# Edge loop of a graph-attention kernel: VectorE adds the gathered rows to the second pair of scores in five of seven steps, and GpSimd's gathers wait for their ring slot alone

## What is computed

```python
src, dst = (edge_index[0], edge_index[1])
x_l = (x @ W_l.T + b_l).reshape(n, HEADS, DIMS)
x_r = (x @ W_r.T + b_r).reshape(n, HEADS, DIMS)
...
e_feat = (e_attr @ W_e.T).reshape(-1, HEADS, DIMS)
s = x_l[src] + x_r[dst] + e_feat
s = jax.nn.leaky_relu(s, NEG_SLOPE)
alpha = jnp.einsum('ehc,hc->eh', s, att)
amax = jax.ops.segment_max(alpha, dst, num_segments=n)
ex = jnp.exp(alpha - amax[dst])
denom = jax.ops.segment_sum(ex, dst, num_segments=n)
alpha = ex / (denom[dst] + 1e-16)
out = jax.ops.segment_sum(alpha[..., None] * x_l[src], dst, num_segments=n)
```

## Time and profile before

| what | value |
|---|---|
| median of 3 launches | 3488.56 us (3485.78 to 3489.42) |
| the profiled execution's own time | 3486.59 us |
| its span, first to last instruction | 3484.9 us |
| scores of the edge loop (L1311), first to last start | 148.5 to 1379.1 us |
| PE busy, share of the span | 3136.0 us, 90% |
| DVE | 1877.1 us, 54% |
| ACT | 1357.1 us, 39% |
| POOL | 1244.5 us, 36% |
| L1311 matmuls, 1680 records | 522.2 us |
| L1312 matmuls, 960 + 720 records | 293.0 + 220.8 us |
| L1294 gathers, 480 + 360 | 461.4 + 345.2 us |

### The profile page before, as it was taken

One profiled execution on the slowest core, in us unless ns is written; L12 is line 12 of the kernel. 1 busy time (PEld: TensorE's weight loads), 2 busy tenths in 40 slices (PEclk: granted clock), 3 DMA queues, 4 the chain that ended last, 5 costly groups with the idle time before them and its releaser, 6 DMA issues. The chain is left out here.

```text
span 3484.9 us, 52064 instructions
## 1 busy us (share of the span) xinstructions
PE 3136.0 (90%) x14323; PEld 2542.8 (73%) x14324; DVE 1877.1 (54%) x3779; ACT 1357.1 (39%) x4647; POOL 1244.5 (36%) x1197
## 2 busy tenths in 40 slices
PE   2799999999999999557998899889989986999988
PEld 1577777777777777346777677767767775888877
DVE  5577877777777877865436343643454340111002
ACT  0047767767777766431223122222312211222232
POOL 2276666666666664113103010300020016000016
PEclk9899999999999999678999999999989978999999
DMA  5576776677676676251101011000000043333333
GB/s 135 155 190 167 168 167 167 164 165 166 166 166 164 166 167 131 78 183 30 30 14 34 23 34 36 8 1 14 27 37 1 1 128 104 113 123 123 115 113 107
DMA packets 301651, 355.64 MB, mean 102 GB/s; under 512 B 164806, under 2 KB 223771, under 8 KB 297545
## 3 DMA queue, kind: packets, MB, share of 16 engines
q0 software_dynamic: 67472, 178.15, 20.1%
q1 hardware_dynamic: 233510, 173.64, 18.8%
q10 hardware_dynamic: 560, 2.35, 0.2%
HBM read 298.03 MB, written 54.91 MB: 101 GB/s over the span
## 5 line engine op out<-in xcount | busy, mean ns | idle before, releaser
L1311 PE MATMUL a_pS<-g_xr,a_lt 128*128 x1680 | 522.2, 393 | 28.0 <-DMA XS<-xl_d,a_ix 22.9
L1294 POOL DMA_INDIRECT a_g<-xl_d,a_ix x480 | 461.4, 961 | 222.4 <-PE a_pS L1312 135.0
L1405 ACT ACTIVATE b_m<-a_g,c_pcx 128x64 f32<-128x64 f32 x1856 | 454.6, 333 | 0.0
L1319 PE MATMUL b_pM<-b_m,b_oh 128*112 128x281 f32 x1680 | 445.3, 404 | 5.3 <-DVE g_acc L1447 3.5
L1440 DVE SCALAR_TENSOR_TENSOR a_r<-a_pS,g_attx 128x528 f32<-128x528 f32 x420 | 296.6, 706 | 243.8 <-PE a_pS L1312 234.8
L1294 POOL DMA_INDIRECT XS<-xl_d,a_ix x360 | 345.2, 959 | 135.3 <-issue 91.5
L113 POOL TENSOR_TENSOR m_rstd<-m_ve,m_mhalf 125x5 f32<-125x5 f32 x45 | 53.1, 1180 | 928.4 <-DVE m_ve L103 919.9
L1311 PEld LDWEIGHTS a_pS<-g_xr,a_lt 128*128 128x128 f32 x1680 | 310.0, 191 | 90.2 <-issue 33.3
L1319 PEld LDWEIGHTS b_pM<-b_m,b_oh 128*112 128x112 f32 x1680 | 292.1, 177 | 102.1 <-issue 11.4
L421 PE MATMUL m_pH<-m_h,m_w 128*128 128x312 f32 (+1 forms) x1280 | 341.9, 428 | 7.7 <-DVE m_h L566 7.7
L1405 ACT ACTIVATE b_m<-XS,c_pcx 128x64 f32<-128x64 f32 x1424 | 348.5, 333 | 0.0
(11 more groups left out here) (371 smaller groups left out, 4410.0 us busy)
## 6 DMA issues: line engine op xcount, KB each, us to landing
a_db<-dl_d SPq DMA_DIRECT2D x212, 224.0 KB
f_w<-in_ffn_W1p SPq DMA_DIRECT2D x32, 1024.0 KB
m_w<-in_mix_W SPq DMA_DIRECT2D x8, 1024.0 KB
f_w<-in_ffn_W2p SPq DMA_DIRECT2D x8, 1024.0 KB
a_g<-xl_d,a_ix POOLq DMA_INDIRECT x480, 5.7
xg_d<-m_zero POOLq DMA_DIRECT2D x1, 7168.0 KB, 30.5
a_lt<-eat_d SPq DMA_DIRECT2D x214, 32.0 KB, 4.1
eat_d<-a_stage SPq DMA_DIRECT2D x15, 448.0 KB
```

The source lines that it names most:

```text
L1294: p.indirect_dma_start(out=gathered(t)[:, j, :], out_offset=None, in_=xl_d, in_offset=bass.IndirectOffsetOnAxis(ap=IX[:, t // BSTEPS, n:n ...
L1311: pe.matmul(o, lt[:, j, :], XRW[:, bass.ds(ws[h], 1), :].rearrange("p a d -> p (a d)"), start=True, stop=False)
L1319: ins = pe.matmul(pM[0:WN, h, 0:MW], OH[:, b, j, :], M[:, b, j, :], start=(j == 2 * h), stop=(j == 2 * h + 1))
L1405: ins = a.activation(m[:, j, part], gathered(ts)[:, j, part], ACT.Copy, scale=of[:, first + j, h, 0:1])
```

## The change

In the steps with tau 2 to 6, `scores(1)` leaves out the identity matmuls of items 2 and 3. VectorE then reads the PSUM pair, adds the gathered rows and writes `R` (`lift`), and later gates `R` in place (`lifted_gate`). The semaphore that lets TensorE write the pair again is given by `lift` (renamed `a_read1`). The two waits of the gathers for scores are gone, with `AHEAD`. The chain at tau 0 and 1, `scores(0)` and `sums` stay.

```diff
-AHEAD = 3
+LIFTED = (2, 3, 4, 5, 6)
...
                         for j in range(IG):
                             n = IG * (t % BSTEPS) + j
-                            if j % 2 == 0:
-                                wait(p, f"a_scored{j // 2}", base, t + 1 - AHEAD)
-                                p.sem_inc(s["a_seen"], 1)
                             p.indirect_dma_start(out=gathered(t)[:, j, :], out_offset=None, in_=xl_d,
...
                         def scores(h, ws):
-                            wait(pe, f"a_gated{h}", base, t)
+                            lifted = h == 1 and t % BSTEPS in LIFTED
+                            wait(pe, f"a_read{h}", base, t)
                             for j in (2 * h, 2 * h + 1):
                                 o = pS[0:TE, j, 0:GD]
-                                pe.matmul(o, lt[:, j, :], XRW[:, bass.ds(ws[h], 1), :].rearrange("p a d -> p (a d)"), start=True, stop=False)
-                                ins = pe.matmul(o, ident[:, :], gathered(t)[:, j, :], start=False, stop=True)
+                                ins = pe.matmul(o, lt[:, j, :], XRW[:, bass.ds(ws[h], 1), :].rearrange("p a d -> p (a d)"), start=True, stop=lifted)
+                                if not lifted:
+                                    ins = pe.matmul(o, ident[:, :], gathered(t)[:, j, :], start=False, stop=True)
...
+                        def lift():
+                            v.wait_ge(s[f"a_g{t}"], 64 * i + 64)
+                            wait(v, "a_scored1", base, t + 1)
+                            v.tensor_tensor(R[:, 2:4, :], pS[0:TE, 2:4, 0:GD], gathered(t)[:, 2:4, :], ALU.add).then_inc(s["a_read1"], 1)
...
+                        def lifted_gate():
+                            wait(v, "a_read1", base, t + 1)
+                            v.scalar_tensor_tensor(out=R[:, 2:4, :], in0=R[:, 2:4, :], scalar=0.0,
+                                                   in1=attx[:, :].unsqueeze(1).broadcast_to([TE, 2, GD]), op0=ALU.max, op1=ALU.mult).then_inc(s["a_gated"], 1)
...
-                        if scoring:
+                        if scoring and lifted:
+                            lift()
+                        elif scoring:
                             gate(1)
...
+                        if scoring and lifted:
+                            lifted_gate()
...
                         if scoring:
-                            wait(v, "a_gated1", base, t + 1)
+                            wait(v, "a_read1", base, t + 1)
+                            if lifted:
+                                v.wait_ge(s["a_gated"], 2 * len(LIFTED) * i + len([k for k in range(t + 1) if k % BSTEPS in LIFTED]))
```

More of the change, by code:

```diff
@@ L1436, in slot @@
                         scores = pA[0:CP, 0:TE]
+                        lifted = t % BSTEPS in LIFTED
+                        def lift():
+                            v.wait_ge(s[f"a_g{t}"], 64 * i + 64)
+                            wait(v, "a_scored1", base, t + 1)
+                            v.tensor_tensor(R[:, 2:4, :], pS[0:TE, 2:4, 0:GD], gathered(t)[:, 2:4, :], ALU.add).then_inc(s["a_read1"], 1)
                         def gate(h):
@@ L1440, in gate @@
                             v.scalar_tensor_tensor(out=R[:, 2 * h:2 * h + 2, :], in0=pS[0:TE, 2 * h:2 * h + 2, 0:GD], scalar=0.0,
-                                                   in1=attx[:, :].unsqueeze(1).broadcast_to([TE, 2, GD]), op0=ALU.max, op1=ALU.mult).then_inc(s[f"a_gated{h}"], 1)
+                                                   in1=attx[:, :].unsqueeze(1).broadcast_to([TE, 2, GD]), op0=ALU.max, op1=ALU.mult).then_inc(s[f"a_read{h}"], 1)
+                        def lifted_gate():
+                            wait(v, "a_read1", base, t + 1)
+                            v.scalar_tensor_tensor(out=R[:, 2:4, :], in0=R[:, 2:4, :], scalar=0.0,
+                                                   in1=attx[:, :].unsqueeze(1).broadcast_to([TE, 2, GD]), op0=ALU.max, op1=ALU.mult).then_inc(s["a_gated"], 1)
                         def add(h, at):
```

## The result

The changed kernel takes 3448.18 us (median of 4, 3447.56 to 3455.33) against 3487.59 for the kernel before (median of 4): the ratio is 0.9892, with a 95% interval of 0.9875 to 0.9909. So it is faster, by 39 us where 85 were forecast. The profiled execution took 3455.33 us, the longest of the four, with a span of 3453.6; that of before was 3486.59, with a span of 3484.9. The gain between the two profiled spans is 31.3 us, less than the 39 of the medians, and all of it lies in the edge loop: the last scores start at 1346.5 us instead of 1379.1.

A forecast was written before the change was run, and what follows sets the result against it. TensorE bounds the kernel; a batch falls from 41.54 to 38.35 us, 28 × 3.19 = 89 us, less 4 for late gathers: 3486.59 less 85 is 3401.6, plus 2 for the median, 3403 us; range 3369 to 3456.

The forecast's parts named there:

- TensorE bound before; ten matmuls a batch, 4.45 us: Edge loop: TensorE sets the pace; ten matmuls at 0.445 us leave each batch, 41.54 to 37.09 us.
- `lift` for the gate, and the lifted gate: VectorE, lifted steps: the lift replaces a gate at 692 ns, adding nothing; the new gate takes 698 ns, adding 3.1 us a batch.
- The half-rate rival: The new gate's two fp32 SBUF inputs stream at half rate, 2.75 us more a batch; 3474 us, chance 0.02.
- VectorE's five steps, 26.1 us: Tau 2 to 6: VectorE needs 25.3 to 26.9 us, middle 26.1, more than TensorE's 24.15.
- The term for the dependence: The reduce must see the finished gate: 0.34 us at tau 4, 5 and 6, 0.7 to 1.2 us a batch.
- The wait at the transpose: Tau 0: TensorE waits for VectorE's reduce before transposing the batch's scores, 1.26 us once a batch.
- The removed waits for scores cost nothing: GpSimd's gathers: their 125.7 us of waits for scores only show GpSimd being ahead, a lead TensorE can't use.
- The gathers: GpSimd supply: 1.26 us a gather, 5.04 a step, 73.1 us a round, against 76.7 forecast for two batches.
- late landings: Gathered rows that arrive late for TensorE: 0.15 us a batch, 4 us in all.
- The place: The narrowest place for gather supply is behind the attribute gathers, at step 2, with 2.1 us to spare.
- The one for supply or clock: Late gathers or a lower TensorE clock after waits take back gain: about 3426 to 3452 us, chance 0.26 together.
- The one of contention between VectorE and GpSimd: SBUF contention lengthens the new gates; at 2.0 us each, 92 us more, 3581 us; chance 0.05.

The follow-up runs named there:

- e5: The changed kernel without the gather of item 3 from the second round on, so three gathers a step; 3387.73 us, ratio 0.9707.
- e1: The kernel before with the gathers' waits for scores taken out and no lift; 3491.78 us, ratio 0.9997.
- r2: The changed kernel with the lift's sum in PSUM and, at tau 2 to 6, the one-hot's node numbers in PSUM; 3396.13 us, ratio 0.9737.
- e3: The changed kernel, but the lift writes its sum back to PSUM and the second gate reads it there; 3404.6 us, ratio 0.9747.
- r1: The kernel of e3 run again, on the same chip as r2; 3409.03 us, ratio 0.9770.
- e4: The kernel before with one more scalar-tensor-tensor at tau 2 to 6, two dense SBUF inputs, result unused; 3492.42 us, ratio 0.9998.
- e6: As e4 on the kernel before, but the added instruction's second input is one column repeated; 3495.85 us in a single run.

## Why the prediction was wrong

**TensorE bound before; ten matmuls a batch, 4.45 us.** Right. Where nothing was late, PE's steps in the changed kernel are as worked out: tau 4 starts at 769.72, tau 5 at 774.86, tau 6 at 779.53, so 5.14 and 4.67 us, each 0.89 less than the like step of before.

**`lift` for the gate, and the lifted gate.** Right. `lift` took 698 ns at the median for 692 forecast, the lifted gate 701 for 698, 716 at most in 150 instances, where the gate with one input in PSUM also has 701. The half-rate rival has gone, and with it, for this form (a scalar-tensor-tensor with two fp32 inputs in SBUF), the rule of the Trainium skill's Vector Engine (DVE) Microarchitecture Reference, section Points that are easy to get wrong.

**VectorE's five steps, 26.1 us.** Too high by 0.9: in the one batch read, from 761.26 to 786.47, they took 25.2 us, just under my low end of 25.3. The term for the dependence was too large:

```profile
774.02 0.70 DVE L1451 SCALAR_TENSOR_TENSOR a_r<-a_r,g_attx 128x528 f32<-128x528 f32 x1
774.76 1.25 DVE L1531 TENSOR_REDUCE a_alpha<-a_r 128x16 f32<-128x1056 f32 x1
```

From the gate's start to the reduce's there are 0.74 us, 0.12 more than the 0.62 of two instructions back to back, where 0.34 were charged. The wait at the transpose exists, 9.2 us in 21 waits in the changed kernel and 16.0 in 26 in e5, against 28 waits of 1.26. In e5, where nothing else is in the way, this error makes the forecast too long by 26 × (1.26 − 0.6) = 17 us; e5's ratio, 0.9707 × 3488.56, gives 3386 where I said 3403.

**The removed waits for scores cost nothing.** Right (e1: 0.9997).

**The gathers: this is the step that failed.** "What counts is the rate: 4 × 1.26 = 5.04 us a step", 73.1 us a round, and 0.15 us a batch for late landings. I took the duration of one gather of before as a constant of GpSimd, although the change puts another SBUF reader on VectorE beside it. The mean is 1.067 us, where the row said 0.95 and the whole loop of before has 0.962. For 56 gathers and 0.305 us between two that makes a round of 79.3 us, where I had 73.1. That is above the 76.7 of my forecast and below the 83.1 of before, so GpSimd became the bound, by 2.6 us a round. Measured from wait to wait the round is 79.8, and over twelve rounds 79.5 where the kernel before has 82.5 (83.1 was twice the one batch that I read). Fourteen rounds at 3.0 us are 42 us; from step 15 to the last scores the trace has 39. The profiled execution gains only 31.3, since at step 15 PE is 6.6 us later than in the kernel before. I had counted no change there. That loss is mostly not from long gathers: r2, with gathers of the old length, is 4.4 us late at the same step. What causes it was not tested.

**The place** was right: the narrow spot is step 2 of the round, behind the attribute gathers. The eight long waits for XS are all there.

**The rivals.** The one for supply or clock, at 3426 to 3452, held the outcome, but by a later landing, and the landing's median fell from 5.7 to 3.6 us. The one of contention between VectorE and GpSimd had the mechanism, and the wrong victim: I priced it on the gate, as a kernel slower than before, and argued it away by the one-hot's own duration. The reading that would have found it was to hand in the trace of before: the longest of 480 gathers there took 1380 ns. Two gathers of before began some 0.05 us into a one-hot, and each took 0.43 us more than 0.945. One of them, on GpSimd's and VectorE's timelines of before:

```profile
583.79 0.61 DVE L1496 TENSOR_TENSOR b_oh<-b_nodes,g_dlx 128x448 f32<-128x448 f32 x1
583.85 1.38 POOL L1294 DMA_INDIRECT a_g<-xl_d,a_ix  x1 [0.30 <-issue]
```

## What to carry to other kernels

When a change gives VectorE an instruction with both inputs in SBUF, price it on GpSimd's queue as well: look at the longest instance of what GpSimd does, not at the VectorE instruction's, and ask in which VectorE instruction it began. Two such instructions back to back are worse for a gather that meets them than one: a gather that began in the one-hot lost 0.650 us in the mean with the lifted gate behind it, and 0.213 in e3 without. In this kernel an operand that lay in PSUM, or was put in free columns there, took away nearly all of the effect and cost VectorE no time: 0.9898 became 0.9737 on one chip. And an engine that is said to have 10 us to spare in 83 should be given its price under the new load, not its old one, before the spare is spent.

## What the runs showed of the hardware that was not expected

- A gather's instruction on GpSimd (0.945 us alone) that begins while VectorE is in an instruction with two SBUF inputs ends later by about what is left of it, or of both where two follow each other, less 0.1 us: the gather of 783.91 lost 0.94 with 1.06 left, that of 779.67 lost 0.40 with 0.53 left. The mean over 73 that began in the one-hot is 0.650 us. The longest gather, 2.26 us, began at 363.18, at the very start of the pair. VectorE's instruction keeps its length, 701 ns at the median and 716 at most. The Trainium skill, GPSIMD Engine Reference, section Specifications, tells of SBUF interfaces that the two share, with contention for VectorE instructions in a 2-port perf mode or with two SBUF inputs; for two SBUF inputs the trace agrees, and here it is GpSimd that pays.
- With one of the two inputs in PSUM the extra is 0.002 to 0.004 us, for the gate and for the one-hot alike; the scans into `c_state` are the exception (0.159 us over 23 gathers before).
- A gather already under way when an instruction with two SBUF inputs starts is not touched: in the kernel before, 177 gathers had a one-hot start 0.01 to 0.93 us after them, and none lost more than 0.02 us. Right at its start it can go either way: in e3 and r1, 21 gathers that began under 0.02 us ahead of the one-hot lost 0.48 to 0.50 us, while two such in e4 lost nothing.
- The size of the second input doesn't matter: one column repeated (e6) gave gathers of 1016 and 983 ns where 528 different columns (e4) gave 1016 and 987. A tensor-scalar instruction with a column as its scalar (`a_lt`) also holds gathers up, by 0.08 to 0.16 us in the mean.
- That the holding up follows from the two inputs is shown by r2 against r1, which moves only the place of one operand, by e3, and by e4, which adds such an instruction and nothing that waits for it. What GpSimd does in that time (whether it is the writing of descriptors or the reading of the indices that waits) was not tried.
